# A wavelet-attention and mixture-of-experts kernel: eleven chunks gathered ahead instead of fourteen, and the first expert's down product one step sooner

## What is computed

```python
scores = jax.nn.sigmoid(h @ gate_w.T)               # 2048 tokens x 16 experts
cap = math.ceil(T / E * TOP_K)                      # 256
topk_score, topk_ids = jax.lax.top_k(scores.T, cap)
xin = h[topk_ids]                                   # 16 x 256 x 128
up = jnp.einsum('ecd,efd->ecf', xin, up_w) + up_b[:, None, :]
g = jnp.einsum('ecd,efd->ecf', xin, gw) + gb[:, None, :]
eo = jax.nn.silu(g) * up
eo = jnp.einsum('ecf,edf->ecd', eo, down_w) + down_b[:, None, :]
flat = (eo * topk_score[..., None]).reshape(-1, Dm)
out = jnp.zeros_like(h).at[topk_ids.reshape(-1)].add(flat)
shared = silu(x @ sh_gate_w.T) * (x @ sh_up_w.T) @ sh_down_w.T
return x + out + shared
```

## Time and profile before

| | us |
|---|---|
| median of 3 runs | 214.91 |
| the three runs | 213.57, 214.91, 215.64 |
| the profiled execution's own time | 213.9 |
| its span (first to last instruction) | 211.9 |

### The profile page before, as it was taken

How to read it: one execution, slowest core, us unless ns; L and a number is a source line. 1 busy time by engine, 2 the same in 40 slices (tenths; PEclk the granted TensorE clock), 3 DMA queues, 4 the chain that set the end, 5 groups by cost and what they waited for, 6 DMA issues and landing times.

```text
span 211.9 us, 3612 instructions
## 1 busy us (share of the span) xinstructions
PE 180.6 (85%) x1198; PEld 156.4 (74%) x1198; DVE 129.4 (61%) x431; ACT 89.9 (42%) x238; POOL 121.6 (57%) x175
## 2 busy tenths in 40 slices
PE   7879889999879898879899999998988999979000
PEld 7857779999736666649699999987977999968000
DVE  4888899999788888788544444443344444444000
ACT  0676603267886864110144444444243444434100
POOL 7510006555144567504777887887887777775550
PEclk9999999999999999999999999999999999999955
DMA  5599999600120650102422332323333233332221
GB/s 135 194 418 419 416 416 419 281 0 3 43 72 0 141 221 2 49 3 57 111 59 66 42 40 40 54 44 44 46 38 38 36 37 42 39 39 25 25 25 12
DMA packets 11617, 22.19 MB, mean 105 GB/s; under 512 B 1488, under 2 KB 8784, under 8 KB 11472
## 3 DMA queue, kind: packets, MB, share of 16 engines
q1 hardware_dynamic: 5968, 17.52, 22.1%
q0 software_dynamic: 5632, 4.46, 15.3%
HBM read 17.65 MB, written 4.33 MB: 104 GB/s over the span
## 4 chain that ended last, share of the span: by engine, by line
PE 32%; DMA 19%; DVE 17%; POOL 12%; issue 10%; ACT 5%; POOLq 1%; SPq 1%; DVEq 0%; ACTq 0%
DMA out_dram<-area,rows 16%; POOL out_dram L486 8%; PE bank L1081 7%; PE bank L1342 4%; PE bank L1343 4%; DVE junk L889 4%; PE bank L1327 3%; PE bank L1036 3%; DMA x_tok<-in_x_dram 2%; POOL sh_hid L460 2%; PE bank L1234 2%; PE bank L1184 2%; ACT area L504 1%; DMA hT<-h_rows,rows 1%; DVE area L740 1%
## 5 line engine op out<-in xcount | busy, mean ns | idle before, releaser
L486 POOL DMA_INDIRECT out_dram<-area,rows x32 | 50.6, 1580 | 16.7 <-DMA out_dram<-area,rows 9.7
L1021 DVE SCALAR_TENSOR_TENSOR area<-bank,consts,sgate 128x256 f32<-128x256 f32 x64 | 30.9, 482 | 38.7 <-ACT sgate L671 38.7
L671 ACT ACTIVATE sgate<-bank,consts 128x256 f32<-128x256 f32 x64 | 30.3, 473 | 56.9 <-PE bank L1343 56.9
L1327 PEld LDWEIGHTS bank<-wT,area 128*128 128x128 f32 x256 | 38.4, 191 | 3.6 <-DVE area L1021 0.4
L1342 PE MATMUL bank<-area,wT 128*128 128x256 f32 x128 | 38.6, 383 | 2.5 <-issue 2.5
L1327 PE MATMUL bank<-wT,area 128*128 128x128 f32 x256 | 38.8, 275 | 0.2 <-DVE area L1021 0.2
L474 POOL DMA_INDIRECT hT<-h_rows,rows x32 | 32.0, 1000 | 11.4 <-issue 9.1
L1343 PE MATMUL bank<-area,wT 128*128 128x256 f32 x128 | 38.1, 379 | 0.0
L1343 PEld LDWEIGHTS bank<-area,wT 128*128 128x128 f32 x128 | 24.3, 190 | 3.3
L460 POOL TENSOR_TENSOR sh_hid<-sh_up,sgate 128x64 f32<-128x64 f32 x48 | 14.4, 336 | 15.8 <-ACT sh_up L627 12.7
L1036 PE MATMUL bank<-ident 128*128 128x128 f32 x152 | 21.5, 298 | 1.6 <-POOL ident L381 1.6
(11 more groups left out here) (186 smaller groups left out, 252.3 us busy)
## 6 DMA issues: line engine op xcount, KB each, us to landing
wT<-in_weights_dram SPq DMA_DIRECT2D x16, 768.0 KB, 16.2
h_rows<-hrow SPq DMA_DIRECT2D x2, 576.0 KB, 3.8
x_tok<-in_x_dram SPq DMA_DIRECT2D x4, 256.0 KB, 4.0
x_tok<-in_down_b_dram SPq DMA_DIRECT2D x1, 1024.0 KB, 6.8
out_dram<-x SPq DMA_DIRECT2D x4, 256.0 KB, 2.4
hT<-h_rows,rows POOLq DMA_INDIRECT x32, 2.6
out_dram<-area,rows POOLq DMA_INDIRECT x32, 3.3
sh_wT<-in_shared_dram SPq DMA_DIRECT2D x1, 384.0 KB, 3.1
```

Source lines behind the costliest of these rows:

```text
L486: pool.indirect_dma_start(out=out_rows, in_=eo[:, e % 2, c, :], in_offset=None, out_offset=bass.IndirectOffsetOnAxis(ap=rows[:, g, c, k:k ...
L671: act.activation(sgate_e[:, q % SGB, :], up_bank(q)[:, CAP:2 * CAP], ACT.Silu, bias=biasT[:, 1, j, e:e + 1]).then_inc(s_sil, 1)
L1021: dve.scalar_tensor_tensor(hidden[:, e % 2, j, :], up_bank(q)[:, 0:CAP], biasT[:, 0, j, e:e + 1], sgate_e[:, q % SGB, :], ALU.add, ALU.mul ...
L1327: last = pe.matmul(bank[3 + e % 2][:, c * P:(c + 1) * P], hidden[:, e % 2, j, c * P:(c + 1) * P], wT[:, e, 2, j, :], start=(j == 0 and c = ...
```

## The change

POOL gathers 11 chunks instead of 14 ahead of its first scatter, and the three that are left out come later: two gathers stand behind each of the first eight scatters (before: six) and one behind each of the next five (before: six). The last gather, chunk 31, stands behind scatter(12) instead of scatter(11).

For the first expert alone the end comes one step sooner: PE issues its last down product, `down(3)`, in step 4 right behind `down(2)`, and none in step 5; DVE adds its bias in step 4 instead of 5; ACT weighs it in step 5 instead of 6. From the second expert on the order is the old one.

```diff
-    AHEAD = 14
-    BETWEEN = (2, 2, 2, 2, 2, 2, 1, 1, 1, 1, 1, 1, 0, 0, 0, 0)
+    AHEAD = 11
+    BETWEEN = (2, 2, 2, 2, 2, 2, 2, 2, 1, 1, 1, 1, 1, 0, 0, 0)
...
-                if j == 2 and e > 0:
+                if (q == FT + 1 or j == 2 and e > 1):
                     weigh(act, e - 1)
...
-                if j == 1 and e > 0:
+                if (q == FT or j == 1 and e > 1):
                     add_bias(e - 1)
...
-                if q >= LAG:
+                if q == FT:
+                    down(q - LAG)
+                    down(q - 1)
+                elif q >= LAG and q != FT + 1:
                     down(q - LAG)
```

## The result

The changed kernel takes 218.96 us (median; 218.05 to 219.40) against 214.27 for the kernel before: the ratio is 1.0229, with a 95% interval of 1.0187 to 1.0271. The change makes the kernel slower by 4.7 us; whether by more than 2%, the interval leaves open. The likeliest class was put as "within 1%", which was wrong.

What follows compares the result with a forecast made beforehand. POOL was taken to set the expert loop's pace; with the change, chunk 31's late gather decides. The sum was 213.9 + 0.21 (later last scatter) + 2.2 (PE's clock falling in the stall) = 216.3 us, range 213.4 to 218.6.

Steps and rivals of the forecast that it cites:

- The likeliest class: Whole kernel's time against the kernel before: same, within 1%, given 0.59; slower 0.37, faster 0.04.
- S(0): Start of the first expert's scatter on POOL: put at 112.15 us, set by POOL and the weighing almost together.
- the gaps up to S(12): Between scatter starts on POOL: eight of 6.425 us, then four of 5.427, putting scatter(12) at 185.26.
- the hand-off from ACT to POOL: From the weighing's first chunk done on ACT to the scatter's start on POOL: 0.1 us allowed.
- S(0) above 113: Sign at the loop's start: a first scatter later than 113 us would show the prediction wrong at the early step.
- turn_x(15): Expert 15's transposes on PE: wait for chunk 31, start at 191.71 us, 6.45 after scatter(12) starts, stalling PE 5.4.
- S(14) - S(13): Gap between the scatter starts of experts 13 and 14 on POOL: over 7 us instead of 5.3.
- the path behind turn_x(15): From expert 15's transposes through PE's work and expert 14's weighing to scatter(14): 6.15 us.
- the clock's price: PE at half pace after its stall for chunk 31: costs 2.2 us, with bounds of nothing and 5.3.
- the rival to which I gave 0.36: In PE's stall ahead of turn_x(15) the clock stays up: 214.1 us, chance 0.36.
- The gain at S(0): First scatter starts earlier than in the kernel before, from 115.79 to 112.15 us: 3.64 us.
- 2.06 given back: Expert loop on POOL: two more two-gather gaps, one fewer with one gather and with none, cost 2.06 us.

Runs made afterwards that it cites:

- e6: Kernel before with eleven chunks gathered ahead and the new gather gaps, without the early step: 220.62 us, ratio 1.0258.
- e2: Kernel before with only chunk 31's gather moved from behind scatter(11) to behind scatter(12): 218.67 us against 215.37, ratio 1.0205.
- e3: Changed kernel with chunks 28 to 31 gathered one gap sooner, chunk 31 again behind scatter(11): 216.08 us, ratio 1.0041.
- e1: Changed kernel run again without any edit, for a second trace: 219.09 us, ratio 1.0189 to the kernel before.
- e8: Changed kernel with 20 more short matmuls on PE at about 84 us, lengthening its instruction stream: 219.33 us, ratio 1.0205.
- e9: Changed kernel run a third time without any edit: ratio 1.0173 to the kernel before.
- e11: Changed kernel with 20 more short matmuls on PE at about 84 us, same kernel as e8, run beside e9: 217.97 us, ratio 1.0148.
- e5: Changed kernel with 40 spare matmuls on PE ahead of turn_x(15): 221.37 us, ratio 1.0274.
- e10: Changed kernel with 20 spare matmuls on PE ahead of turn_x(15): 217.50 us, ratio 1.0119.
- e4: Kernel before with the early step alone, fourteen chunks ahead and old gather gaps: 215.51 us against 215.37, ratio 1.0017.

## Why the prediction came out as it did

The steps that failed are S(0) and the gaps up to S(12). S(0) was put 14.49 us behind the first gather and came at 16.81; S(12) was put at 87.60 and came at 91.74. Behind that stand one term that was too small, the hand-off from ACT to POOL, and two that were put at nothing: PE's own delay, which the fourteen gathers had covered, and late landings. By the prediction's own sign, S(0) above 113, it was wrong at the early step; yet that step came and saved its 0.86 us (e6), and what made S(0) late was the rest.

**Right: the mechanism.** Chunk 31 became the wait that ends last, at the place forecast: turn_x(15) 6.41 behind S(12) (6.45 forecast). S(14) - S(13) is 9.33, and 9.37 was forecast (197.86 + 2.2 - 190.69), but that this is so near is luck: the path behind turn_x(15) was 0.61 us longer than I had it, the clock's price was 1.5 instead of 2.2, and the two errors cancel. In the other traces with the stall it is 9.0 to 10.4. e2 and e3 show that this one gather is the loss: added alone it costs 2.05%, put back it leaves 0.41% of the 1.89%.

**Right: the clock falls.** It fell in all seven traces that have the stall without spare matmuls (the first one, e1, e2, e6, e8, e9, e11), so the rival to which I gave 0.36, a clock that stays up, did not occur. Its price varies. S(14) comes behind turn_x(15) by:

| trace | low clock after turn_x(15), us | S(14) - turn_x(15), us |
|---|---|---|
| e5 and e10 | 0 | 6.73 and 6.79 |
| e11 | 2.7 | 8.11 |
| e2 | 2.8 | 8.13 |
| after | 3.0 | 8.25 |
| e1 | 3.6 | 8.55 |
| e9 | 4.1 | 8.79 |
| e8 | 4.8 | 9.12 |
| e6 | 5.4 | 9.43 |

That is 6.76 and half of the time at the lower level, within 0.1: a price of 1.4 to 2.7 us, around the 2.2 taken from the kernel's start. The Trainium skill, "TensorE: Matmul & The Clock Gate", section "What's actually happening", has the place of a change shift from run to run, because what watches the activity runs freely. The traces agree on the shifting: the fall came 2.2 us (e1) to 4.9 (e6) after PE went quiet. It never came late enough to spare the kernel. The single 4.0 of the earlier trace rows was a fair guide here, but not as the lower end.

**Wrong: the hand-off from ACT to POOL.** I put 0.1 us between the weighing and the scatter, from the earlier trace rows and the scatter that started 0.12 behind a weighing (POOL's timeline before):

```profile
194.19 1.55 POOL L486 DMA_INDIRECT out_dram<-area,rows  x1 [0.30 <-ACT area L504]
```

That is the second scatter of expert 13, and the weighing that ended at 194.07 is that of expert 14, which it doesn't need. POOL was not waiting for ACT there; the nearness was an accident. Where POOL does wait, it takes 0.75 to 0.84: in the changed kernel the first expert's weighing,

```profile
112.42 0.68 ACT L504 ACTIVATE area<-area,hT 128x128 f32<-128x128 f32 x2
```

has its first chunk done at about 112.82, and S(0) is 113.66. The last stall shows it too (202.50 to 203.25). The term came in twice: S(0) is 15.25 after the first gather in a trace without the low clock near 96 us (e1, e3, e9, e11), where 112.15 - 97.66 = 14.49 was forecast, and turn_x(15) to S(14) has 6.76 where I had 6.15. Together 1.4 us. The weighings themselves came as forecast: the first one in e1 started 14.01 us behind the first gather (13.99 forecast). The gain at S(0) is thus 18.13 - 15.25 = 2.88 instead of 3.64, and the 2.06 given back nearly eat it.

**Left out: what fourteen gathers covered.** The low clock near 96 us makes PE 1.57 us late: turn_x(1) is 10.84 to 10.86 behind the first gather with it, 9.27 to 9.28 without. It is there in 4 of 13 traces, with the old schedule (e4) and the new. With the old, POOL's gathers hide it; with eleven, S(0) waits for PE, and the 1.57 go straight into S(0). I looked at the cover of each step that the change moves, and not at what the removed gathers had covered.

**Left out: landings that aren't alike.** I took each gap's length from a mean. A second scatter that has an instruction fetch beside it can land in 4.2 to 5.3 us instead of 3.3, and the next scatter waits for it. In the earlier trace rows the fetches met first scatters, at 159.83 and 176.20 (4.2 and 4.5 us to landing), which nobody waits for, so the means were those of a lucky trace. In the changed kernel's first trace two met second scatters: 0.39 and 1.46 us.

The balance for the changed kernel's first trace, from its first gather to S(15), in which 2.4 more than before were forecast and 6.4 came: hand-off at S(0) 0.75, low clock near 96 us 1.57, landings and the small differences of the gaps 1.72, the stall -0.04 (its two errors cancel, as said). These are the 4.0 missing; 0.8 of them the run got back by an earlier start. In e1, without the low clock near 96, 3.0 are missing: 0.76, 2.11, and 0.12 at the end.

**The chances.** The step from a sum to classes was poor as well. 216.3 lay on the border between "same" and "slower", and I let the rival with the clock up pull the weight to "same". What I had left out were waits, and they could only add.

## What to carry to other kernels

When work is taken away ahead of a wait, ask two things: what else that work was covering, and which later transfer is now the last one before its own deadline; each buffer's fill has a last slot in the schedule, and one slot later, by itself, cost here as much as the whole change (2.05% against 1.89%). A hand-off between two engines is priced only from a place where the receiver really waits; an instruction that happens to start just behind another is no price.

## What the runs showed of the hardware that I had not expected

An accumulating scatter of one chunk usually lands 3.3 us after its issue. The 16 second scatters that landed late took 4.2 to 5.3, each beside a 0.02 MB instruction fetch that started 1.9 to 3.3 us after the scatter's issue; a fetch that started earlier went with so late a landing only once (4.45, e3). In the changed kernel the one issued at 172.75 took:

```profile
DMA to landing us min/median/max: 4.8/4.8/4.8
```

The Trainium skill, "Runtime: NRT & Kernel Launch", section "Instruction fetch mechanics", calls the cost of crossing from one fetched block of instructions into the next mostly hidden. Whether it is for the engine that runs them, no run here shows; for a kernel whose chain runs through the landing of a DMA, the traces speak against it, as far as coincidence can: gaps of 6.8 to 7.5 us (e4 and e11 among them), instead of 5.5 or 6.4, where a fetch falls beside the transfer.

Where POOL waits for it, its start behind ACT takes 0.75 to 0.84 us; its start behind a landing takes 0.27 (the "issue" step of the chain), and 0.30 lie between two of its own indirect transfers.
